# Score maxima from block-diagonal bf16 keys: one 128-row product for two heads, in place of two 64-row products

## The chip, the cores and the metric

The kernel runs on one core of one Trainium2 chip. The metric is the device time of one execution in microseconds. Engines are named as in the profile: PE (TensorE matmul), PEld (TensorE weight load), DVE (VectorE), ACT (ScalarE), POOL (GpSimd), SP (SyncE, which only issues DMAs here).

## The reference

Two layers of cross attention and feed-forward on x of 32 x 128 x 128, with a context of 32 x 77 x 128. Only the first attention is touched by the change: 16 heads of width 64, rotary embedding on queries and keys, a mask of 128 x 77 per batch.

```
Q = (q @ Wq).reshape(b, ql, 16, 64)
K = (k @ Wk).reshape(b, kl, 16, 64)
V = (v @ Wv).reshape(b, kl, 16, 64)
Q, K = (rope(Q), rope(K))
attn = jnp.einsum('bqhd,bkhd->bhqk', Q / scale, K)
attn = jnp.where(mask[:, None, :, :] == 0, -INF, attn)
attn = jax.nn.softmax(attn, axis=-1)
out = jnp.einsum('bhqk,bkhd->bqhd', attn, V).reshape(b, ql, 16 * 64)
return out @ Wo
```

## The kernel before

The program is written out by hand, engine by engine, with semaphores. The first attention takes the 32 batches in 16 pairs. A pair p has two slots, one for each of its batches (j = 0 and j = 1); `pairs_loop` writes out pairs 0 and 1, loops over pairs 2 to 13 (two pairs to a turn of the loop), and writes out pairs 14 and 15. The order of work on each engine is fixed by the text of its `slot`. While pair p is being attended to, the queries, keys and values of pair p + 1 are projected.

Channels lie on partitions: a tile of 128 partitions holds two heads, the even one on partitions 0 to 63 and the odd one on 64 to 127; there are 8 tiles.

Scores are computed twice. First in bf16, `score_maxima(b)`, with queries on the rows, only to find each row's maximum: three PSUM banks first receive the mask through three products with the identity (`am`, line 986, over 308, 462 and 462 columns), then 16 products (line 995) add the scores, one for each head, 64 rows by 128 columns of weights (`qb`) and 77 moving columns (`kb`). Even and odd heads are interleaved so that two 64-row products stand side by side. The bank of four heads gets both parities, so its second half waits for its first (`half_done`). DVE then takes the maxima, bank by bank (`maxima`, line 736: two of 6 heads, one of 4). PE transposes them (`turn_maxima`, line 1007), ACT copies the result (`fold`, line 862), and the fp32 scores (`scores`, lines 1017 and 1021) subtract mask and maximum through a product with `fold`.

The bf16 operands are made by ACT: `cast_queries` (line 850) and `cast_keys` (line 858), from the fp32 `qr` and `kr`. For the keys of pair p + 1, all in the slot j = 1 of pair p: PE projects them in three groups of 3, 3 and 2 tiles (line 970); DVE multiplies and shuffles (lines 679, 681); POOL makes `kr` of the groups 0 and 1 (lines 592, 593), having first made the last group of queries (lines 580, 581), whose PSUM input PE produced at the end of the slot j = 0; DVE makes `kr` of the group 2 (line 724); ACT casts each group as it comes, in order. PE goes through the rest of the slot (`scores`, `turn_out`, `out_projection`, `values`, and `project_values(p + 1, 1)`, lines 949 to 951) and then, before `score_maxima` of the next pair's first batch, executes

```
pe.wait_ge(cast_done, 3 * p + 6)
```

that is, it waits for the third cast of the pair. In the prologue the same wait stands ahead of `score_maxima(0)`. Behind it on PE come `score_maxima`, `project_values`, the transposes of pair p + 2, `turn_out`, `turn_maxima`, and the next slot. Line 845 (ACT) copies projected values out of PSUM, behind the casts in ACT's order.

At the start, POOL sets five small constants (lines 561 to 563) and DVE and ACT wait for the semaphore `setup` to reach 5 before their first work.

Of the kernel before, what the change touches and what calls it, by code (L numbers as in the profile page):

```python
# [11 lines left out]
BF16 = mybir.dt.bfloat16  # L12
# [6 lines left out]
B, S, D, KL = 32, 128, 128, 77  # L19
# [3 lines left out]
TILES = H0 * DK0 // 128  # L23
# [4 lines left out]
CROW = 96  # L28
# [373 lines left out]
def layer0_attention(nc, ctx, t):  # L402

    sb = lambda name, shape, dt: ctx.enter_context(nc.sbuf_tensor("a0_" + name, shape, dt))
# [8 lines left out]
    am = [sb(f"am{i}", [S, 2, FOLD], BF16) for i in range(2)]  # L413
# [12 lines left out]
    kr = [sb(f"kr{i}", [128, TILES, 2, KL], F32) for i in range(2)]  # L426
    qb_all = sb("qb", [128, 2 * TILES * 2 * S], BF16)
    qb = [qb_all[:, 2048 * i:2048 * i + 2048].rearrange("p (t j s) -> p t j s", t=TILES, j=2) for i in range(2)]
    kb = [sb(f"kb{i}", [128, TILES, 2, KL], BF16) for i in range(2)]
    vs = [sb(f"vs{i}", [KL, 2, H0, DK0 + 1], F32) for i in range(2)]  # L430
    fold = sb("fold", [FOLD, S], BF16)
    probs = sb("probs", [KL, H0, S], F32)
# [16 lines left out]
    pa, ps, po = bank[0:2], bank[2:5], bank[5:8]  # L449
# [4 lines left out]
    setup = sem("setup")  # L454
    stats_ready, rstd_ready, xhat_ready = sem("stats_ready"), sem("rstd_ready"), sem("xhat_ready")
    a_full, a_free = [sem(f"a_full{i}") for i in range(2)], [sem(f"a_free{i}") for i in range(2)]
    s_full, s_free = [sem(f"s_full{i}") for i in range(3)], [sem(f"s_free{i}") for i in range(3)]
    values_full, normalised, turned_full, turned_in, out_full, out_added = (
        sem(n) for n in ("values_full", "normalised", "turned_full", "turned_in", "out_full", "out_added"))
    roped, k_roped, cast_done, half_done = sem("roped"), sem("k_roped"), sem("cast_done"), sem("half_done")  # L460
# [11 lines left out]

    SM_BANK = (1, 2, 0)
    SM_COUNT = (lambda b: 2 * b, lambda b: 2 * b, lambda b: 4 * b)
    SM_HEADS = ((0, 2, 4, 6, 8, 10), (1, 3, 5, 7, 9, 11), (12, 14, 13, 15))
    SM_ORDER = ((2, 0), (1, 0), (2, 1), (1, 1), (0, 0), (1, 2), (0, 1), (1, 3), (0, 2), (1, 4), (0, 3), (1, 5),
                (0, 4), (2, 2), (0, 5), (2, 3))

    FOLD_COUNT = lambda b: 4 * b + 1
    ST_BANK = (0, 1, 2, 0)  # L480
# [39 lines left out]
    def a_count(p, task):  # L520

        return 6 * p + task[1] + 1 - task[0]
# [35 lines left out]
    def gpsimd(pool, second):  # L558
        steps = Steps(pool, pool_step)
        for i in range(2):  # L560
            nc.gpsimd.memset(am[i][:, :, KL:CROW], 0.0).then_inc(setup, 1)
            nc.gpsimd.memset(vs[i][:, :, :, DK0:DK0 + 1], 1.0).then_inc(setup, 1)
        nc.gpsimd.memset(t["minus_half"][:], -0.5).then_inc(setup, 1)
        pool.wait_ge(setup, 5)

        def pre(p):
            pool.wait_ge(stats_ready, p + 1)
# [51 lines left out]
    def vector(dve, second):  # L619
# [107 lines left out]
        def maxima(b, P, j):  # L727
            for m in range(3):
                bk = SM_BANK[m]
                dve.wait_ge(s_full[bk], SM_COUNT[m](b) + 1)  # L730
                n, first = len(SM_HEADS[m]), CROW + SM_HEADS[m][0]
                if m < 2:
                    rows = am[P][:, j, first:first + 2 * n - 1:2]
                else:
                    rows = am[P][:, j, first:first + 4].rearrange("p (i e) -> p e i", e=2)
                nc.vector.tensor_reduce(rows, ps[bk][:, 0:n * KL].rearrange("p (h k) -> p h k", k=KL),  # L736
                                        AX, ALU.max).then_inc(s_free[bk], 1)

# [15 lines left out]
            nc.vector.tensor_tensor(x[:, b, :], po[2][:, 0:D], x[:, b, :], ALU.add).then_inc(out_added, 1)  # L754

        dve.wait_ge(x_first_in, 16)
        dve.wait_ge(setup, 5)
        masks(0, 0)
        statistics(0)
        normalised_rows(0)  # L760
# [22 lines left out]
        def slot(b, p, P, j, more):  # L783
# [24 lines left out]
            else:  # L808
# [15 lines left out]
                if more:  # L824
                    maxima(b + 1, 1 - P, 0)
# [9 lines left out]
    def scalar(act, second):  # L835
# [16 lines left out]
        def cast_keys(p, P, k):  # L852
            if k < 2:
                act.wait_ge(k_roped, 2 * p + k + 1)
            else:
                act.wait_ge(a_free[K_TASK[k][0]], a_count(p, K_TASK[k]) + 1)
            lo, hi = K_GROUPS[k]
            nc.scalar.copy(kb[P][:, lo:hi], kr[P][:, lo:hi]).then_inc(cast_done, 1)  # L858

        def fold_in(b):  # L860
            act.wait_ge(s_full[0], FOLD_COUNT(b) + 1)
# [14 lines left out]
        act.dma_start(*x_chunk(0)).then_inc(x_first_in, 16)  # L876
        act.dma_start(t["ident"][:], t["c_id"]).then_inc(t["ids_in"], 16)
        act.dma_start(t["identb"][:], t["c_idb"]).then_inc(t["ids_in"], 16)
        act.wait_ge(setup, 5)
        nc.scalar.activation(t["front"].first_silu[0:S, :], t["minus_half"][:, 0:1], ACT.Exp)  # L880
        act.wait_ge(first_weights_in, 32)
        nc.scalar.copy(wq_hi[:], wq[:]).then_inc(weights_split, 1)
# [54 lines left out]
    def tensor(pe, second):  # L937
# [43 lines left out]

        def score_maxima(b, P, j):
            for m in (2, 0, 1):
                bk, n = SM_BANK[m], len(SM_HEADS[m])
                pe.wait_ge(s_free[bk], SM_COUNT[m](b))
                nc.tensor.matmul(ps[bk][:, 0:n * KL].rearrange("p (h k) -> p h k", k=KL), t["identb"][:],  # L986
                                 am[P][:, j:j + 1, 0:KL].broadcast_to([S, n, KL]), start=True, stop=False,
                                 skip_group_check=True)
            for m, i in SM_ORDER:
                h = SM_HEADS[m][i]  # L990
                e = 64 * (h % 2)
                if (m, i) == (2, 2):

                    pe.wait_ge(half_done, b + 1)
                last = nc.tensor.matmul(ps[SM_BANK[m]][:, i * KL:i * KL + KL], qb[P][e:e + 64, h // 2, j, :],  # L995
                                        kb[P][e:e + 64, h // 2, j, :], start=False, stop=True, skip_group_check=True)
                if (m, i) == (2, 1):
                    last.then_inc(half_done, 1)
                if i == len(SM_HEADS[m]) - 1:
                    last.then_inc(s_full[SM_BANK[m]], 1)  # L1000

        def turn_maxima(b, P, j):

# [132 lines left out]
        out_projection(B - 1)  # L1136

    return dict(sync=sync, gpsimd=gpsimd, vector=vector, scalar=scalar, tensor=tensor)


# [980 lines left out]
```

## Time and profile before

| what | value |
|---|---|
| three runs | 737.15, 739.62, 739.86 us; median 739.62 us |
| span of the profiled execution, first to last instruction | 736.9 us |
| median of the runs less that span | 2.7 us |
| PE busy | 94% of the span |
| DVE, ACT, POOL busy | 76%, 55%, 55% |
| mean granted TensorE clock | 0.993 |

The profiled execution has no time of its own beside its span in what is shown; the 2.7 us by which the runs' median exceeds it is what lies before the first and behind the last instruction, and the spread of the runs. Times below are microseconds from the span's start unless marked ns.

### The profile page before, as it was taken

How to read it: one execution, taken by the hardware profiler on the slowest of the kernel's cores; microseconds unless marked ns; L12 is line 12 of the kernel's file. 1: busy time of each engine (PE TensorE's matmuls, PEld its weight loads, DVE VectorE, ACT ScalarE, POOL GpSimd, SP SyncE). 2: the span in 40 equal slices, each digit the busy share in tenths (PEclk: the TensorE clock that was granted, in tenths of full speed). 3: DMA queues.
4: the chain of work that ended last, by engine and by line, in shares of the span. 5: the costliest groups of instructions: out<-in, count | busy, mean ns of one | idle time of the engine just before them, and what ended most of it. 6: DMA issues, size and time to landing. Idle time of an engine off the chain costs nothing.

```text
span 736.9 us, 24302 instructions
## 1 busy us (share of the span) xinstructions
PE 695.7 (94%) x9267; PEld 574.1 (78%) x9272; DVE 561.1 (76%) x1633; ACT 407.2 (55%) x902; POOL 403.7 (55%) x496
## 2 busy tenths in 40 slices
PE   3789999999999999999999999999999999997785
PEld 3578888888888888888888887788888888875544
DVE  5676786786786786787787675777887888887996
ACT  2344554544544544545544544556666766766896
POOL 3474574484484474475466452546556565633775
PEclk9899999999999999999999999999999999999999
DMA  9400000000000000000000000000000000000011
GB/s 264 115 9 12 9 3 11 10 0 9 9 0 9 9 0 9 9 0 9 9 0 0 1 2 11 10 7 11 7 9 4 9 4 4 5 2 1 22 44 52
DMA packets 23682, 13.04 MB, mean 18 GB/s; under 512 B 6560, under 2 KB 22768, under 8 KB 23632
## 3 DMA queue, kind: packets, MB, share of 16 engines
q1 hardware_dynamic: 22816, 12.00, 6.1%
q8 instruction: 33, 0.54, 0.3%
q10 hardware_dynamic: 816, 0.36, 0.2%
q14 instruction: 17, 0.14, 0.1%
HBM read 10.25 MB, written 2.10 MB: 17 GB/s over the span
## 4 chain that ended last, share of the span: by engine, by line
PE 83%; DVE 9%; issue 3%; ACT 3%; DMA 1%; POOL 0%; ACTq 0%; SPq 0%; DVEq 0%
PE bank L1017 9%; PE bank L1033 9%; PE bank L1053 8%; PE bank L1648 6%; PE bank L949 5%; PE bank L1021 5%; PE bank L970 4%; PE bank L1681 4%; PE bank L951 4%; PE bank L950 4%; PE bank L1044 4%; PE bank L986 2%; PE bank L1666 2%; PE bank L995 2%; DVE f_h_max L1898 2%
## 5 line engine op out<-in xcount | busy, mean ns | idle before, releaser
L580 POOL TENSOR_TENSOR a_turned<-a_turned,a_rope 128x512 f32<-128x512 f32 x63 | 80.7, 1280 | 175.8 <-DVE a_turned L668 175.8
L867 ACT ACTIVATE a_probs<-bank 77x512 f32<-77x512 f32 x128 | 70.8, 590 | 64.9 <-PE bank L1021 64.0
L845 ACT COPY a_vs<-bank 77x512 f32<-77x512 f32 x64 | 37.4, 584 | 101.5 <-PE bank L951 101.5
L665 DVE TENSOR_TENSOR a_straight<-bank,a_rope 128x512 f32<-128x512 f32 x63 | 43.4, 689 | 58.3 <-PE bank L951 54.5
L581 POOL TENSOR_TENSOR a_qr<-a_straight,a_turned 128x512 f32<-128x512 f32 x64 | 82.3, 1286 | 4.9
L1017 PE MATMUL bank<-a_qr,a_kr 64*77 64x128 f32 x1024 | 71.4, 279 | 2.2 <-ACT a_probs L867 0.3
L1017 PEld LDWEIGHTS bank<-a_qr,a_kr 64*77 64x77 f32 x1024 | 56.5, 145 | 16.4 <-ACT a_fold L862 8.6
L1033 PE MATMUL bank<-a_vs,a_probs 77*64 77x65 f32 x2048 | 67.0, 223 | 0.4 <-DVE x_all L754 0.4
L1033 PEld LDWEIGHTS bank<-a_vs,a_probs 77*64 77x64 f32 x2048 | 62.4, 137 | 4.5 <-DVE x_all L754 0.6
L1053 PE MATMUL bank<-a_wo,a_oTn 128*128 128x128 f32 x512 | 64.0, 278 | 0.0
L736 DVE TENSOR_REDUCE a_am<-bank 128x6 bf16<-128x462 f32 (+1 forms) x96 | 50.3, 581 | 14.2 <-PE bank L995 14.2
L1053 PEld LDWEIGHTS bank<-a_wo,a_oTn 128*128 128x128 f32 x512 | 59.9, 192 | 1.0
L850 ACT CAST a_qb<-a_qr 128x512 bf16<-128x512 f32 x64 | 39.4, 618 | 23.5 <-POOL a_qr L581 23.2
L668 DVE STREAM_SHUFFLE a_turned<-bank 128x512 f32<-128x512 f32 x63 | 46.2, 733 | 0.0
L970 PE MATMUL bank<-a_ctxT,a_wk 128*128 128x154 f32 x256 | 45.0, 312 | 0.7 <-ACT a_vs L845 0.7
L1380 DVE TENSOR_REDUCE a_max_m<-bank 128x8 f32<-128x512 f32 x64 | 41.1, 684 | 5.1 <-PE bank L1629 4.6
L1518 ACT ACTIVATE a_qr<-bank 128x512 f32<-128x512 f32 (+1 forms) x96 | 43.8, 538 | 1.0 <-PE bank L1666 1.0
L949 PE MATMUL bank<-a_xT_hi,a_wq_hi 128*128 128x256 f32 x128 | 40.0, 313 | 3.0 <-DVE a_turned L668 1.6
L1021 PE MATMUL bank<-a_fold,a_fold_w 112*77 112x128 bf16 x512 | 41.1, 223 | 0.0
L593 POOL TENSOR_TENSOR a_kr<-a_k_straight,a_k_turned 128x462 f32<-128x462 f32 x32 | 38.5, 1202 | 4.3 <-DVE a_k_turned L688 1.9
L858 ACT CAST a_kb<-a_kr 128x462 bf16<-128x462 f32 (+1 forms) x48 | 24.2, 533 | 27.8 <-POOL a_kr L593 27.7
L873 ACT COPY a_oTn<-bank 128x512 f32<-128x512 f32 x64 | 35.5, 582 | 7.2 <-PE bank L1044 7.2
(277 smaller groups left out, 1890.2 us busy)
## 6 DMA issues: line engine op xcount, KB each, us to landing
out<-x_all SPq DMA_DIRECT2D x16, 128.0 KB, 1.8
x_all<-in_x_dram SPq DMA_DIRECT2D x7, 256.0 KB, 6.5
a_ctx_in<-in_ctx SPq DMA_DIRECT2D x16, 77.0 KB
a_mask_in<-in_mask SPq DMA_DIRECT2D x16, 77.0 KB
a_wv<-in_ctx SPq DMA_DIRECT2D x16, 77.0 KB
a_wq<-in_Wq SPq DMA_DIRECT2D x1, 512.0 KB, 4.9
a_wk<-in_Wk SPq DMA_DIRECT2D x1, 512.0 KB, 6.3
a_wv<-in_Wv SPq DMA_DIRECT2D x1, 512.0 KB, 7.2
```

The source lines that it names most:

```text
L580: steps.link(nc.gpsimd.tensor_tensor(tv, tv, rope[:, 1:2, :].broadcast_to([128, 4, S]), ALU.mult))
L581: nc.gpsimd.tensor_tensor(qr[P][:, 2 * k:2 * k + 2, :, :].rearrange("p t j s -> p (t j) s"), sv, tv, ALU.subtract if made else ALU.add).th ...
L668: nc.vector.stream_shuffle(turned[k % 3][:], pv, mask=[lane ^ 1 for lane in range(32)]).then_inc(a_free[bk], 1)
L736: nc.vector.tensor_reduce(rows, ps[bk][:, 0:n * KL].rearrange("p (h k) -> p h k", k=KL), AX, ALU.max).then_inc(s_free[bk], 1)
L867: nc.scalar.activation(probs[:, 4 * g:4 * g + 4, :], ps[ST_BANK[g]][0:KL, :].rearrange("p (h s) -> p h s", s=S), ACT.Exp).then_inc(s_free[ ...
L949: nc.tensor.matmul(out, lhs_hi, rhs_hi, start=True, stop=False)
L970: last = nc.tensor.matmul(pa[bk][:, 2 * KL * i:2 * KL * i + 2 * KL], wk[:, 128 * (lo + i):128 * (lo + i) + 128], ctxT[:], start=True, stop ...
L1017: nc.tensor.matmul(ps[ST_BANK[g]][0:KL, i * S:(i + 1) * S], kr[P][e:e + 64, h // 2, j, :], qr[P][e:e + 64, h // 2, j, :], start=i == 0, st ...
L1021: last = nc.tensor.matmul(ps[ST_BANK[g]][0:KL, i * S:(i + 1) * S], fold_w[:, h, :], fold[:], start=False, stop=True, skip_group_check=True)
L1033: last = nc.tensor.matmul(po[r][rows, VW * i:VW * (i + 1)], probs[:, PROBS_SLOT[h], rows], vs[P][:, j, h, :], start=True, stop=True)
L1053: last = nc.tensor.matmul(po[2][:, 0:D], oTn[:, i, :], wo[:, i, :], start=i == 0, stop=i == TILES - 1)
L1648: return nc.tensor.matmul(SCORES[g][:, i * S:(i + 1) * S], keys[P][FEATURES[half], j, 128 * tile:128 * tile + 128], q1[P][FEATURES[half], ...
```

## The change

The bf16 keys `kb` become block diagonal: for each tile, a first block of 77 columns holds the even head's keys on partitions 0 to 63 and zero below, and a second block holds zero above and the odd head's keys on partitions 64 to 127. One product of 128 rows by 154 columns then gives both heads' scores. The 16 products of a batch become 8, the banks hold consecutive heads, and the three banks are finished one after the other instead of together. `half_done` is no longer waited for. Each cast of keys becomes two, one for each half of the partitions. POOL sets both `kb` buffers to zero once at the start (128 partitions by 2464 bf16 elements each), ahead of `setup` reaching 7.

```diff
-    kb = [sb(f"kb{i}", [128, TILES, 2, KL], BF16) for i in range(2)]
+    kb = [sb(f"kb{i}", [128, TILES, 2, 2, KL], BF16) for i in range(2)]
...
-    SM_HEADS = ((0, 2, 4, 6, 8, 10), (1, 3, 5, 7, 9, 11), (12, 14, 13, 15))
...
+    SM_TILES = (range(0, 3), range(3, 6), range(6, 8))
...
+            nc.gpsimd.memset(kb[i][:], 0.0).then_inc(setup, 1)
         nc.gpsimd.memset(t["minus_half"][:], -0.5).then_inc(setup, 1)
-        pool.wait_ge(setup, 5)
+        pool.wait_ge(setup, 7)
...
-                n, first = len(SM_HEADS[m]), CROW + SM_HEADS[m][0]
-                if m < 2:
-                    rows = am[P][:, j, first:first + 2 * n - 1:2]
-                else:
-                    rows = am[P][:, j, first:first + 4].rearrange("p (i e) -> p e i", e=2)
+                first, n = CROW + 2 * SM_TILES[m][0], 2 * len(SM_TILES[m])
+                rows = am[P][:, j, first:first + n]
...
-            nc.scalar.copy(kb[P][:, lo:hi], kr[P][:, lo:hi]).then_inc(cast_done, 1)
+            for e in range(2):
+                last = nc.scalar.copy(kb[P][64 * e:64 * e + 64, lo:hi, :, e, :], kr[P][64 * e:64 * e + 64, lo:hi])
+            last.then_inc(cast_done, 1)
...
-            for m, i in SM_ORDER:
-                h = SM_HEADS[m][i]
-                e = 64 * (h % 2)
-                if (m, i) == (2, 2):
-
-                    pe.wait_ge(half_done, b + 1)
-                last = nc.tensor.matmul(ps[SM_BANK[m]][:, i * KL:i * KL + KL], qb[P][e:e + 64, h // 2, j, :],
-                                        kb[P][e:e + 64, h // 2, j, :], start=False, stop=True, skip_group_check=True)
-                if (m, i) == (2, 1):
-                    last.then_inc(half_done, 1)
-                if i == len(SM_HEADS[m]) - 1:
-                    last.then_inc(s_full[SM_BANK[m]], 1)
+            for m in range(3):
+                for i, tile in enumerate(SM_TILES[m]):
+                    last = nc.tensor.matmul(ps[SM_BANK[m]][:, 2 * KL * i:2 * KL * i + 2 * KL], qb[P][:, tile, j, :],
+                                            kb[P][:, tile, j].rearrange("p e k -> p (e k)"), start=False, stop=True,
+                                            skip_group_check=True)
+                last.then_inc(s_full[SM_BANK[m]], 1)
```

## Rows read from the trace of the kernel before

**Rows 1.** The page: busy times, and the chain that ended last by engine.

```profile
PE 695.7 (94%) x9267; PEld 574.1 (78%) x9272; DVE 561.1 (76%) x1633; ACT 407.2 (55%) x902; POOL 403.7 (55%) x496
...
PE 83%; DVE 9%; issue 3%; ACT 3%; DMA 1%; POOL 0%; ACTq 0%; SPq 0%; DVEq 0%
```

**Rows 2.** Chain that ended last, 134 to 145 us: start, us, what.

```profile
141.14 0.48 PE bank L995 x16
```

**Rows 3.** Timeline by form, 138.5 to 144.5 us (start, duration, engine, line).

```profile
137.78 1.18 POOL L593 TENSOR_TENSOR a_kr<-a_k_straight,a_k_turned 128x462 f32<-128x462 f32 x1
...
138.99 0.93 ACT L858 CAST a_kb<-a_kr 128x462 bf16<-128x462 f32 x2 [1.70 <-POOL a_kr L593]
...
140.43 0.24 PEld L986 LDWEIGHTS bank<-a_am,identb 128*128 128x128 bf16 x3 [0.32 <-issue]
140.44 0.70 PE L986 MATMUL bank<-a_am,identb 128*128 128x308 bf16 x3
...
141.07 0.55 PE L995 MATMUL bank<-a_kb,a_qb 64*128 64x77 bf16 x16
...
141.54 0.45 PE L949 MATMUL bank<-a_wv_hi,a_ctxT_hi 128*77 128x512 f32 x1
...
141.62 1.57 DVE L736 TENSOR_REDUCE a_am<-bank 128x6 bf16<-128x462 f32 x3 [0.52 <-PE bank L995]
...
143.52 0.22 PE L1007 MATMUL bank<-identb,a_am 128*112 128x128 bf16 x1
```

**Rows 4.** Timeline, 128.9 to 131.2 us: what starts POOL's run.

```profile
131.01 1.27 POOL L580 TENSOR_TENSOR a_turned<-a_turned,a_rope 128x512 f32<-128x512 f32 x1 [0.75 <-DVE a_turned L668]
```

**Rows 5.** Groups by form, ACT line 858: busy us, mean ns, idle before.

```profile
L858 ACT CAST a_kb<-a_kr 128x462 bf16<-128x462 f32 x32 | 18.5, 577 | 27.7 <-POOL a_kr L593 27.7
...
L858 ACT CAST a_kb<-a_kr 128x308 bf16<-128x308 f32 x16 | 7.1, 443 | 0.1
```

**Rows 6.** Chain, 476 to 480 us: bf16 products of full height, 128 columns.

```profile
478.22 0.56 PE bank L1666 x10
```

**Rows 7.** Timeline, 112.3 to 113.6 us: the pair before.

```profile
111.98 0.93 ACT L858 CAST a_kb<-a_kr 128x462 bf16<-128x462 f32 x2 [1.70 <-POOL a_kr L593]
...
113.37 0.50 PE L986 MATMUL bank<-a_am,identb 128*128 128x308 bf16 x2
```

**Rows 8.** Timeline, 57 to 58.9 us: batch 2, written out.

```profile
57.14 0.93 ACT L858 CAST a_kb<-a_kr 128x462 bf16<-128x462 f32 x2 [1.70 <-POOL a_kr L593]
...
58.57 0.50 PE L986 MATMUL bank<-a_am,identb 128*128 128x308 bf16 x2
```

**Rows 9.** Timeline, 84 to 86.5 us: batch 4.

```profile
84.04 1.12 ACT L858 CAST a_kb<-a_kr 128x462 bf16<-128x462 f32 x2 [1.60 <-POOL a_kr L593]
...
86.31 0.50 PE L986 MATMUL bank<-a_am,identb 128*128 128x308 bf16 x2
```

**Rows 10.** Timeline, 27.5 to 30.2 us: batch 0, the prologue.

```profile
27.87 1.00 ACT L858 CAST a_kb<-a_kr 128x462 bf16<-128x462 f32 x2 [1.20 <-POOL a_kr L593]
...
28.93 0.70 PE L986 MATMUL bank<-a_am,identb 128*128 128x308 bf16 x3 [1.81 <-ACT a_kb L858]
```

**Rows 11.** Groups, POOL, 0 to 2 us: the memsets of the start.

```profile
L562 POOL MEMSET a_vs<- 77x32 f32 x2 | 0.3, 151 | 0.0
L561 POOL MEMSET a_am<- 128x38 bf16 x2 | 0.3, 128 | 0.3 <-POOLq L2110 0.3
L2110 POOL MEMSET const-bfloat16-1.0<- 128x1 bf16 x1 | 0.1, 101 | 0.0
```

**Rows 12.** Timeline, 0 to 62 us: the start on POOL and DVE.

```profile
0.98 0.10 POOL L563 MEMSET minus_half<- 128x4 f32 x1
...
4.61 0.24 DVE L625 TENSOR_SCALAR a_am<-a_mask_in 128x154 bf16<-128x154 int32 x1 [4.61 <-DMA a_mask_in<-in_mask]
...
10.03 0.42 DVE L655 TENSOR_TENSOR a_xT_lo<-bank,a_xT_hi 128x256 fp32r<-128x256 f32 x1
```

**Rows 13.** Line 736: who waited for it (us, times).

```profile
  PE bank L1007: 2.2, 3
```

**Rows 14.** Stretches: busy us by engine, PEclk, DMA.

```profile
30.00:36.60 6.60, 6.17 (x31) 3.92 (x29) 3.07 (x9) 1.55 (x5) 0.07 (x1) 0.50 0.15 41
```

More of the change, by code:

```diff
@@ L474, in layer0_attention @@
     SM_COUNT = (lambda b: 2 * b, lambda b: 2 * b, lambda b: 4 * b)
-    SM_HEADS = ((0, 2, 4, 6, 8, 10), (1, 3, 5, 7, 9, 11), (12, 14, 13, 15))
-    SM_ORDER = ((2, 0), (1, 0), (2, 1), (1, 1), (0, 0), (1, 2), (0, 1), (1, 3), (0, 2), (1, 4), (0, 3), (1, 5),
-                (0, 4), (2, 2), (0, 5), (2, 3))
+    SM_TILES = (range(0, 3), range(3, 6), range(6, 8))
     FOLD_COUNT = lambda b: 4 * b + 1
@@ L756, in vector @@
         dve.wait_ge(x_first_in, 16)
-        dve.wait_ge(setup, 5)
+        dve.wait_ge(setup, 7)
         masks(0, 0)
@@ L878, in scalar @@
         act.dma_start(t["identb"][:], t["c_idb"]).then_inc(t["ids_in"], 16)
-        act.wait_ge(setup, 5)
+        act.wait_ge(setup, 7)
         nc.scalar.activation(t["front"].first_silu[0:S, :], t["minus_half"][:, 0:1], ACT.Exp)
@@ L983, in score_maxima @@
             for m in (2, 0, 1):
-                bk, n = SM_BANK[m], len(SM_HEADS[m])
+                bk, n = SM_BANK[m], 2 * len(SM_TILES[m])
                 pe.wait_ge(s_free[bk], SM_COUNT[m](b))
```

## The prediction, made before the change was run

> **What bounds the kernel now.** I read the page first: PE is busy 94% of the span, and the chain that ended last is 83% PE [rows 1]. Then the chain in order of time through a settled pair: from 60 us to 436 us it is nearly all PE, and the products that the change replaces stand on it in every batch [rows 2]. So in the first attention a nanosecond on PE, or a wait of PE, costs a nanosecond. Next I looked for what PE nearly waits for. The timeline of one pair [rows 3] shows two near misses: the third cast of the keys ends at 138.99 + 0.93 = 139.92 and PE takes up line 986 at 140.44, 0.52 later; the maxima end at 141.62 + 1.57 = 143.19 and PE takes up line 1007 at 143.52, 0.33 later. The reader should see in the first that ACT starts the second cast 0.03 after POOL's row ends (137.78 + 1.18 = 138.96), having idled 1.70 before it: ACT has time, but not at that place.
>
> **PE's own work.** Now, from line 986's first start to the product behind line 995 is 141.54 - 140.44 = 1.10, of which line 995 takes 0.47 and line 986 0.63 [rows 3]. Full-height bf16 products of 128 columns go at 0.56/10 = 0.056 each, 0.44 ns a column [rows 6]. The identity products have 308 + 462 + 462 = 1232 columns, 0.54 at that rate; the 0.09 left is lost where full height gives way to 64 rows. Afterwards nothing changes height: 0.54 + 8 x 154 columns (0.54) = 1.08 against 1.10. With rounding I take -0.03 a batch, x 32 = -1.0. Bounds: 0 to -0.06 a batch (the second if all of the 0.09 and some of the like at the far end comes back on top), so 0 to -2, unless the loss at the change of height stays (a rival below).
>
> The Trainium skill (TensorEngine Tiling (Array Packing), Key Properties) says that a change of tiling mode drains the array; the 0.09 agrees. The same skill speaks against the change (TensorE: Matmul & The Clock Gate, Why this matters for your kernels): products of few rows in separate row groups run concurrently. By concurrency alone the 16 products would be 8 x 77 columns, 0.27, and the new ones 0.54: +0.27 a batch, +8.6 in all. The row gives them 0.47 with losses at the edges, so most of that price is paid already.
>
> **The casts.** Three casts a pair (577, 577, 443 ns, rows 5) become six. Halving the partitions halves no free dimension: each half still streams 462 or 308 elements a partition, so I take the full duration for each. Two casts in a row overlap by 577 + 443 - 930 = 90 ns [rows 3, 5]. Group 0 is doubled in ACT's idle 1.70 and costs nothing. Groups 1 and 2 cannot start before POOL's kr: the last of four casts ends (577 - 90) + (443 - 90) = 0.84 later. I use 0.83. Does the cover of 0.52 hold? PE needs some time from the cast's end to line 986. In the prologue, where it really waited, it was 28.93 - 28.87 = 0.06 [rows 10]. In the loop the wait's threshold, and those of the three waits behind it, are worked out by the sequencer between; the weight load of line 986 shows 0.32 of "issue" ahead of it [rows 3]. I take 0.20, between the two and nearer the second since the loop's code is that of the second row. Stall = 0.83 + 0.20 - cover. The cover is 0.52 in one pair and 113.37 - 112.91 = 0.46 in the next [rows 3, 7], alternating through the loop: 0.51 and 0.57, mean 0.54. Twelve pairs of the loop: +6.5. Bounds with 0.06 and 0.32: 0.40 and 0.66 a pair, 4.8 and 7.9.
>
> Outside the loop: batch 2 has a cover of 58.57 - 58.07 = 0.50 and thresholds that are constants, so 0.83 + 0.06 - 0.50 = +0.4 [rows 8]. Batch 4 has 86.31 - 85.16 = 1.15: nothing [rows 9]; batch 30 looks like it: nothing. Batch 0 waits already: +0.8 less some 0.05 because its third cast now starts behind DVE's kr: +0.75 [rows 10].
>
> Is such a stall won back? Behind the waiting PE stand the maxima, the values, turn_out, the next slot, hence the query projections of the next pair. POOL's run that ends in kr starts from a DVE shuffle of the last query group, after an idle 0.75 [rows 4], and DVE waits there for PE. So the late side hangs on PE as well: all slides together, and the next pair stalls again. Casts that run 0.83 longer push the copy of values (line 845) too, but PE's projection that it waits for ends later than the casts do. Not won back.
>
> **The maxima.** The first bank is full after 3 products of 8 instead of at the end, so DVE starts some 0.25 earlier. Line 1007 waited for DVE 3 times in the whole run, 2.2 in total [rows 13]; elsewhere PE comes 0.33 later anyway [rows 3]. I count one batch: -0.25. Bounds 0 and -0.75.
>
> **The start.** Two memsets of 2464 bf16 a partition go ahead of `setup`. Nearest row: 38 elements of bf16 in 128 ns against 1 element in 101 ns: 0.73 ns an element; the strided f32 one gives (151 - 101)/31 = 1.6 [rows 11]. Hence 1.9 to 4.1 each; the first is the same instruction and type, and I take 2.1. POOL's constants ended at 1.08; now at 5.3. DVE's first work starts at 4.61, released by a DMA [rows 12]: +0.7 late. Does it pass on? At 10.03 DVE subtracts xT_hi as soon as it has it, and PE's first projection waits for that; the path through DVE's first rows, PE's transposes and ACT's three casts ends there with no slack. So +0.7. Bounds: +0.3 and +4.7.
>
> **Sum.** -1.0 + 6.5 + 0.4 + 0.75 - 0.25 + 0.7 = +7.1. On the profiled span, 736.9 + 7.1 = 744.0; the runs' median lies 2.7 above that span, and 739.6 + 7.1 = 746.7, which I predict.
>
> **The rivals.**
> 1. *The casts stay hidden* (not slower). If a cast on 64 partitions costs half, or the six overlap better, the last ends less than 0.26 to 0.32 later (cover less 0.20), and that is the point from which it decides. For it: ACT is 45% idle, and no row shows a cast on 64 partitions at partition 64. Against it: 577 ns for 462 columns and 443 for 308 show that the time goes by columns. Time: -1.0 - 0.25 + 0.7 + 0.2 = about 739.3, no change. Chance 0.12.
> 2. *The array's change of height still costs*, or the concurrency of the old products was worth more than the rows let me see: the 0.09 and its like at the far end stay, +0.12 a batch rather than -0.03, so +4.8 on the forecast: 751.5. Against it: three full-height products follow one another at the column rate. Chance 0.06.
> 3. *The start costs most*: memsets at 1.6 ns an element (+4.0), or the later work meets the clock differently: in 30.0 to 36.6 us the granted clock was at the lower level, 1.2 GHz, 6.6 long, after PE had idled before line 986 [rows 10, 14], and another half of such a stretch would cost 1.7 to 3.3. 749 to 751. Chance 0.09.
> 4. *The maxima were on the path after all*: the 0.25 counts in every batch, 31 x 0.25 = 7.8 back, and the casts' loss is cancelled: 739. Against it: rows 13. Chance 0.04.
>
> The forecast itself, 743.5 to 749, keeps 0.65; 0.04 is for a gain I don't see.
>
> **How the numbers follow.** A measurement of this kernel can tell about 0.5%, 3.7 us, from no change; three runs before spread over 2.7. Slower by more than that is above 743.3: the forecast (0.65 less a little, for its lower edge with a low run), rivals 2 and 3 and nothing else, 0.79. Same: rivals 1 and 4 and that lower edge, 0.17. Faster: 0.04. The range: low bounds of all terms give -2 + 4.8 + 0.4 + 0.75 - 0.75 + 0.3 = +3.5, 743.1, less 1.6 for a low draw of the runs: 741.5. High: 7.9 in the loop, no gain on PE, +1 at the start, +10.0, 749.7; with a part of rival 3, 751.
>
> **What would show it.** Casts of 64 partitions at 577 and 443 ns, six a pair; PE's line 986 with an idle of about 0.5 released by ACT a_kb in 12 pairs of the loop, about 0.4 at batch 2, none at batches 4 and 30; the 8 products 0.067 apart, with 1.07 to 1.08 from line 986 to the next line; the period of a pair up from 27.07 (140.44 - 113.37, rows 3, 7) to about 27.55; DVE's first row near 5.3. It is wrong if the half casts take 300 ns, if PE shows no idle at line 986, or if the sequencer's 0.20 is 0.

## The result and the profile after

| | before | changed |
|---|---|---|
| median of 6 runs each, us | 739.79 (737.15 to 743.01) | 747.77 (747.09 to 749.23) |
| span of the profiled execution, us | 736.9 | 745.3 |
| mean granted TensorE clock | 0.993 | 0.995 |

The ratio is 1.0108, with a 95% interval of 1.0081 to 1.0136: 8.0 us slower. The prediction was 746.7 us, +7.1. Two of its terms were off, in opposite directions, and half cancel. Executions of one kernel also differ in the clock: three of the changed kernel's took 747.1 to 747.3 us at a mean granted clock of 0.995, and two took 749.2 at 0.985.

The page of the changed kernel, against [rows 1]:

```profile
span 745.3 us, 23821 instructions
PE 694.7 (93%) x9016; PEld 579.4 (78%) x9016; DVE 561.2 (75%) x1633; ACT 434.5 (58%) x950; POOL 407.9 (55%) x498
PE 38%; issue 26%; POOL 24%; DVE 9%; ACT 3%; POOLq 1%; ACTq 0%; DVEq 0%
```

PE was 83% of the chain and is 38% of it now, though PE's busy time fell by only 1.0 us. POOL has 24% where it had none: PE now waits, pair after pair, for something that leads back through ACT to POOL. That does not make POOL the engine that bounds the kernel: it is busy 55% as before, and the 26% of "issue" are mostly POOL's own idle time between the pairs (10.89 us from 139.61 in the chain of this pair). ACT's busy time is up by 27.3.

The timeline of the changed kernel over the same place of the same pair as [rows 3] (start, duration, engine, line; in brackets the idle time before and what ended it):

```profile
139.24 1.18 POOL L592 TENSOR_TENSOR a_kr<-a_k_straight,a_k_turned 128x462 f32<-128x462 f32 x1
140.45 2.12 ACT L855 CAST a_kb<-a_kr 64x462 bf16<-64x462 f32 x4 [1.10 <-POOL a_kr L592]
141.66 0.40 PE L949 MATMUL bank<-a_wv_hi,a_ctxT_lo 128*77 128x512 f32 x1
142.59 0.58 ACT L841 COPY a_vs<-bank 77x512 f32<-77x512 f32 x1
142.69 0.25 PEld L984 LDWEIGHTS bank<-a_am,identb 128*128 128x128 bf16 x3 [1.11 <-issue]
142.69 0.70 PE L984 MATMUL bank<-a_am,identb 128*128 128x308 bf16 x3 [0.64 <-ACT a_kb L855]
143.63 1.57 DVE L732 TENSOR_REDUCE a_am<-bank 128x6 bf16<-128x462 f32 x3 [1.08 <-PE bank L989]
143.73 0.44 PE L947 MATMUL bank<-a_wv_hi,a_ctxT_hi 128*77 128x512 f32 x1
```

Line 984 is line 986 of before, 989 is 995, 855 is 858. Three readings. The four casts behind POOL's row take 2.12 where the two took 0.93: 1.19 more. PE starts line 984 at 142.69, 0.12 after the casts end (140.45 + 2.12 = 142.57). And from the start of line 949 to line 984 there is 1.03. Where PE waits for nothing, as in batch 30, written out behind the loop, that is 446.53 - 446.30 = 0.23:

```profile
446.30 0.40 PE L949 MATMUL bank<-a_wv_hi,a_ctxT_lo 128*77 128x512 f32 x1
446.53 0.70 PE L984 MATMUL bank<-a_am,identb 128*128 128x308 bf16 x3
```

So the stall is 1.03 - 0.23 = 0.80 (0.81 as the mean of the loop's twelve pairs), not the 0.64 in the bracket, which counts from a modelled end of line 949. The count of who ended the idle time at line 984 (us and times, of which 14 times are PE's own and 4 the weight loads') and the casts by form (busy, mean ns, idle before), against [rows 5]:

```profile
  ACT a_kb L855: 16.2, 18
```

```profile
L855 ACT CAST a_kb<-a_kr 64x462 bf16<-64x462 f32 x64 | 37.2, 581 | 18.5 <-POOL a_kr L592 18.2
L855 ACT CAST a_kb<-a_kr 64x308 bf16<-64x308 f32 x32 | 14.4, 451 | 0.6
```

The pair's period, from the same line two pairs in a row:

```profile
115.00 0.70 PE L984 MATMUL bank<-a_am,identb 128*128 128x308 bf16 x3 [0.66 <-ACT a_kb L855]
...
170.38 0.70 PE L984 MATMUL bank<-a_am,identb 128*128 128x308 bf16 x3 [0.65 <-ACT a_kb L855]
```

142.69 - 115.00 = 27.69 and 170.38 - 142.69 = 27.69, against 140.44 - 113.37 = 27.07 [rows 3, 7]. Over the loop, from batch 6 to batch 28, the means are 27.70 and 27.05 (before, 27.03 and 27.07 take turns).

### The profile page after: what moved, and what is told of

Read it like the earlier page. It is cut to its first block, busy times and chain, and to the rows that moved or that the text cites. A ratio compares the mean times of both kernels' runs of the same rounds, so it can differ in the third digit from the quotient of the medians.

```text
span 745.3 us, 23821 instructions
## 1 busy us (share of the span) xinstructions
PE 694.7 (93%) x9016; PEld 579.4 (78%) x9016; DVE 561.2 (75%) x1633; ACT 434.5 (58%) x950; POOL 407.9 (55%) x498
## 4 chain that ended last, share of the span: by engine, by line
PE 38%; issue 26%; POOL 24%; DVE 9%; ACT 3%; POOLq 1%; ACTq 0%; DVEq 0%
POOL a_turned L579 9%; POOL a_qr L580 8%; PE bank L1640 5%; PE bank L1673 4%; POOL a_k_turned L591 4%; PE bank L1658 2%; DVE f_h_max L1890 2%; POOL a_kr L592 2%; PE bank L1009 2%; PE bank L1045 1%; PE bank L1614 1%; PE bank L1025 1%; PE bank L1599 1%; PE bank L1704 1%; PE bank L1691 1%
## 5 line engine op out<-in xcount | busy, mean ns | idle before, releaser
L732 DVE TENSOR_REDUCE a_am<-bank 128x6 bf16<-128x462 f32 (+1 forms) x96 | 50.3, 579 | 18.8 <-PE bank L989 17.2
L855 ACT CAST a_kb<-a_kr 64x462 bf16<-64x462 f32 (+1 forms) x96 | 51.6, 538 | 19.1 <-POOL a_kr L592 18.2
L1510 ACT ACTIVATE a_qr<-bank 128x512 f32<-128x512 f32 (+1 forms) x96 | 43.8, 538 | 1.0 <-PE bank L1658 1.0
```

Source lines behind the costliest of these rows:

```text
L855: last = nc.scalar.copy(kb[P][64 * e:64 * e + 64, lo:hi, :, e, :], kr[P][64 * e:64 * e + 64, lo:hi])
L1510: nc.scalar.activation(probs[:, 4 * g:4 * g + n, :], SCORES[g].rearrange("p (t s) -> p t s", s=S), ACT.Exp).then_inc(s_free[g], 1)
```

## The experiments

The theory on trial is the prediction's: PE's new products cost no more than the old ones, and all the loss in the loop is PE waiting at the head of the maxima for a longer chain of casts. The rivals: the new products or the clock cost time, the loss is in the start, or the casts would have been hidden. Chain, stall and period in the table are in us and are means over the loop. The chain is the time from the start of the first cast behind POOL's last kr to the end of the last one. The period is that from line 984 (or its like) to the next pair's, the stall is taken as above.

| | chain of casts behind POOL's kr | stall | period | ratio to before |
|---|---|---|---|---|
| before | 0.93 | 0 | 27.05 | |
| changed | 2.12 | 0.81 | 27.70 | 1.0108 |
| e1, three full casts, new products | 0.94 | 0 | 26.89 | 0.993 |
| e2, old products, full casts twice | 1.76 | 0.47 | 27.54 | 1.0085 |
| e3, old products, casts in halves | 2.09 | 0.80 | 27.86 | 1.0142 |
| e7, changed, halves in another order | 1.87 | 0.58 | 27.47 | 1.0082 |
| e4, changed, DVE casts the odd halves, memsets moved | 0.94 | 0 | 26.89 | 0.9932 |
| e6, as e4, memsets not moved | 0.94 | 0 | 26.89 | 0.9947 |
| e5, changed, memsets moved | 2.11 | 0.83 | 27.71 | 1.0127 |
| e8, changed again | 2.11 | 0.82 | 27.71 | 1.0114 |

In the loop the granted clock is 1.00 in every kernel's profile, so chain, stall and period can be compared directly. The ratios also hold what happens near the start, where PE spends some stretches at 1.2 GHz that differ from kernel to kernel; the texts on e1, e2, e3 and e5 give them.

### e1: the new products with the old casts

Each cast is one instruction again and fills the even block on all partitions; the odd block stays zero. What comes out are maxima of the sum of two heads' scores, so this kernel leaves out the separation of heads; PE's instructions are those of the changed kernel.

```diff
-            for e in range(2):
-                last = nc.scalar.copy(kb[P][64 * e:64 * e + 64, lo:hi, :, e, :], kr[P][64 * e:64 * e + 64, lo:hi])
-            last.then_inc(cast_done, 1)
+            nc.scalar.copy(kb[P][:, lo:hi, :, 0, :], kr[P][:, lo:hi]).then_inc(cast_done, 1)
```

> The changed kernel with one cast of full height per group of keys, into the even block only (the odd heads' block stays zero and the even block's lower half holds the odd head's keys, so the maxima are those of a sum of two heads). The products, the banks and the memsets stay as changed. Theory A (the loss is the chain of casts behind POOL's last kr): in the loop no wait of PE for the keys, period of a pair 27.07 less the gain of the products, which in the changed kernel's rows is 1.11 - 1.03 and 1.11 - 1.07, so about 26.95; with 0.75 of start kept, 0.998 of the kernel before, 738 us. Rival B (the loss lies in the products of full height or in the memsets and the clock after them): the time stays near the changed kernel's, 1.011 of before, 747 to 748 us.

Measured 735.19 us (734.74 to 737.58) against 740.61, ratio 0.993 [0.9903, 0.9957]: faster than the kernel before, and by more than expected. The timeline of e1:

```profile
136.13 1.18 POOL L592 TENSOR_TENSOR a_kr<-a_k_straight,a_k_turned 128x462 f32<-128x462 f32 x1
137.34 0.93 ACT L854 CAST a_kb<-a_kr 128x462 bf16<-128x462 f32 x2 [1.68 <-POOL a_kr L592]
138.78 0.70 PE L982 MATMUL bank<-a_am,identb 128*128 128x308 bf16 x3
```

The casts end at 138.27 and PE comes 0.51 later without a wait, the cover of [rows 3]. The target's stride (blocks of 77 in 154) costs next to nothing: 0.93 here, 0.94 in the mean of the loop, where it was 0.93. The period is 0.17 shorter than before, so the products are a gain of 0.17 a pair, some 2.7 us over 16 pairs.

That is half of the 5.4 us between the medians. The profiled span is 3.6 shorter than before's (733.3 against 736.9), although PE's first projection comes 0.76 later; at batch 1, behind a single round of products, e1 is already 1.59 ahead. What the rows show to differ there is the clock: e1's PE runs at 1.2 GHz from 18.3 to 25.1 and from 28.5 to 31.9, before's from 29.9 to 36.7. The rest of the 5.4 lies in before's other executions: three of the twelve, at a mean granted clock of 0.979, took 743.4 us, and the three at 0.990 or 0.993 took 738.2 to 739.4.

### e2 and e3: the old products with more casts

e2 casts each group twice at full height, the second time into a tile that nothing reads.

```diff
+    kx = [sb(f"kx{i}", [128, TILES, 2, KL], BF16) for i in range(2)]
...
-            nc.scalar.copy(kb[P][:, lo:hi], kr[P][:, lo:hi]).then_inc(cast_done, 1)
+            nc.scalar.copy(kb[P][:, lo:hi], kr[P][:, lo:hi])
+            nc.scalar.copy(kx[P][:, lo:hi], kr[P][:, lo:hi]).then_inc(cast_done, 1)
```

> The kernel before, with each cast of keys followed by a second one of full height from the same source into an unused tile; nothing else changes, output as the reference. Theory A: slower. If a second cast follows the first as closely as group 2 followed group 1 before (0.48 after 577 ns, that is 90 ns of overlap), the third group ends 0.84 later, PE stalls about 0.48 in 12 pairs of the loop, +7, ratio 1.009. If two casts in a row don't overlap, as in the changed kernel, 1.19 later, stall about 0.83, +11 to 12, ratio 1.015 to 1.017. Rival B: no change, since the products are the old ones: within 0.3%.

e3 casts each group in two halves of the partitions, into the old layout.

```diff
-            nc.scalar.copy(kb[P][:, lo:hi], kr[P][:, lo:hi]).then_inc(cast_done, 1)
+            for e in range(2):
+                last = nc.scalar.copy(kb[P][64 * e:64 * e + 64, lo:hi], kr[P][64 * e:64 * e + 64, lo:hi])
+            last.then_inc(cast_done, 1)
```

> The kernel before, with each cast of keys cut into two of 64 partitions each, written without gaps into the old tile; output as the reference. It separates the height of a cast from the strided target: if 64 partitions at a time (or the second at partition 64) is what removes the overlap, casts start 0.58 to 0.60 apart here and in the changed kernel, but 0.48 apart in the run with doubled casts of full height; if it is the strided target, here they start 0.48 apart. Theory A: +11 to 12 us (1.015) in the first case, +7 (1.009) in the second. Rival B: no change.

e2: 747.13 us (745.45 to 749.82), ratio 1.0085 [1.0054, 1.0116]. e3: 751.76 (749.36 to 753.95), 1.0142 [1.0111, 1.0173]. The same number of casts, of the same duration each, and yet 4.6 us apart. The timeline of ACT in e2, and PE's line 988 behind it:

```profile
142.69 0.58 ACT L859 CAST a_kb<-a_kr 128x462 bf16<-128x462 f32 x1 [1.22 <-POOL a_kr L594]
143.17 0.57 ACT L860 CAST a_kx<-a_kr 128x462 bf16<-128x462 f32 x1
143.65 0.45 ACT L859 CAST a_kb<-a_kr 128x308 bf16<-128x308 f32 x1
144.00 0.44 ACT L860 CAST a_kx<-a_kr 128x308 bf16<-128x308 f32 x1
144.35 0.57 ACT L846 COPY a_vs<-bank 77x512 f32<-77x512 f32 x1
...
144.58 0.70 PE L988 MATMUL bank<-a_am,identb 128*128 128x308 bf16 x3 [0.30 <-ACT a_kx L860]
```

And of e3:

```profile
143.15 2.09 ACT L859 CAST a_kb<-a_kr 64x462 bf16<-64x462 f32 x4 [1.11 <-POOL a_kr L593]
...
145.37 0.70 PE L988 MATMUL bank<-a_am,identb 128*128 128x308 bf16 x3 [0.63 <-ACT a_kb L859]
```

In e2 a cast starts 0.48 after the one before, though that lasts 0.58: they overlap by 0.09, and the four end 1.76 after the first starts (1.75 by the rounded rows), 0.83 more than two do. That is the prediction's figure, and in e2 it holds. In e3 the four take 2.09. They start 0.59, 0.60 and 0.46 apart: no overlap at any change from one half of the partitions to the other. e3 has the changed kernel's chain without its products, and its period and ratio are the highest of all.

The two medians also hold something that is not the casts. Both profiled executions have a second stretch at 1.2 GHz, from 43.6 to 50.4 in e2 and from 43.8 to 50.6 in e3, where the kernel before has none. A window of e2:

```profile
43.60:50.40 6.80, 6.80 (x78) 6.00 (x79) 2.89 (x8) 1.55 (x4) 3.26 (x3) 0.50 0.01 2
```

Before's granted clock in it is 1.00. From batch 1 to batch 2 both fall behind before by 3.57 (in e3 0.70 of it is a stall for the casts at batch 2; in e2 PE waits there for DVE instead). From batch 0 to batch 1 both had gained 1.4, with a first stretch of 3.4 in place of 6.8. So of the 9.2 by which e2's span is longer than before's, the stalls of the loop are 5.8. The theory rests on the periods, not on how near the ratios came to what was expected.

The Trainium skill (ScalarE: Activation LUTs, What ACT_TABLE_LOAD costs) gives an activation with immediate scale and bias 186 ns + 0.833 ns an element and says that ones back to back overlap by about 93 ns. e2's rows agree with both (571 and 443 ns by it, 0.09 overlap); the halves of e3 agree with the duration (577 and 449 ns for the first of each group) and not with the overlap, and there the measurement decides.

### e7: one change of half in place of three

The four casts behind POOL's row in the order group 1 lower, group 2 lower, group 2 upper, group 1 upper.

```diff
+        def cast_half(p, P, k, e):
+            lo, hi = K_GROUPS[k]
+            return nc.scalar.copy(kb[P][64 * e:64 * e + 64, lo:hi, :, e, :], kr[P][64 * e:64 * e + 64, lo:hi])
...
-            for e in range(2):
-                last = nc.scalar.copy(kb[P][64 * e:64 * e + 64, lo:hi, :, e, :], kr[P][64 * e:64 * e + 64, lo:hi])
-            last.then_inc(cast_done, 1)
+            if k == 2:
+                return
+            act.wait_ge(k_roped, 2 * p + k + 1)
+            cast_half(p, P, k, 0)
+            if k == 1:
+                act.wait_ge(a_free[K_TASK[2][0]], a_count(p, K_TASK[2]) + 1)
+                cast_half(p, P, 2, 0)
+                cast_half(p, P, 2, 1).then_inc(cast_done, 1)
+            cast_half(p, P, k, 1).then_inc(cast_done, 1)
```

> The changed kernel, with the last four casts of a pair in the order even half of group 1, even half of group 2, odd half of group 2, odd half of group 1. The same six casts on ACT and the same data; only the number of changes from one half of the partitions to the other falls from three to one. Theory A2 (two casts in a row overlap by 90 ns as long as both lie on the same half; a change of half costs the overlap and a little more, which is why my 0.84 became 1.19): starts 0.49, 0.46 and 0.35 apart in place of 0.60, 0.60 and 0.47, last end 1.88 behind POOL's kr in place of 2.15, the stall down by about 0.25 a pair, 3 to 4 us less than the changed kernel: 1.006 to 1.007 of before. Rival A3 (casts of 64 partitions never overlap): starts 0.58 to 0.60 apart, no difference to the changed kernel, 1.011.

745.6 us (743.81 to 746.54), ratio 1.0082 [1.0056, 1.0108]; the changed kernel, run again beside it (e8), 747.62 and 1.0114. The timeline of e7:

```profile
139.63 1.87 ACT L850 CAST a_kb<-a_kr 64x462 bf16<-64x462 f32 x4 [1.10 <-POOL a_kr L592]
...
141.63 0.70 PE L989 MATMUL bank<-a_am,identb 128*128 128x308 bf16 x3 [0.39 <-ACT a_kb L850]
```

The same four instructions in another order take 1.87 in place of 2.12, and starts at 0.49 (no change of half), 0.46 (change, behind a cast of 0.45) and 0.355 (no change) apart. So it is the change of half that loses the overlap. PE's period falls by 0.23 with it (27.70 to 27.47).

The copy of values that ACT does behind the casts, on 77 partitions from partition 0, shows which property counts. In e2 it follows a cast on all 128 partitions and starts 0.09 before that ends (144.35, against 144.00 + 0.44). In the changed kernel it follows a cast on partitions 64 to 127 and starts 0.02 behind its end (142.59 against 142.57). Two instructions of different height overlap where both start at partition 0, so these rows speak for the first partition, not the height.

### e4: the odd halves of the late groups on DVE

```diff
...
-            for e in range(2):
+            for e in range(2) if k == 0 else (0,):
                 last = nc.scalar.copy(kb[P][64 * e:64 * e + 64, lo:hi, :, e, :], kr[P][64 * e:64 * e + 64, lo:hi])
...
+        def cast_odd_keys(p, P):
+            for k in (1, 2):
+                if k == 1:
+                    dve.wait_ge(k_roped, 2 * p + 2)
+                else:
+                    dve.wait_ge(a_free[K_TASK[2][0]], a_count(p, K_TASK[2]) + 1)
+                lo, hi = K_GROUPS[k]
+                nc.vector.tensor_copy(kb[P][64:128, lo:hi, :, 1, :], kr[P][64:128, lo:hi]).then_inc(odd_cast, 1)
...
                     pe.wait_ge(cast_done, 3 * p + 6)
+                    pe.wait_ge(odd_cast, 2 * p + 4)
```

DVE does this behind `residual` in the slot j = 1, and PE waits for `odd_cast` too. The memsets of `kb` were also moved behind POOL's constants, under a semaphore of their own (e5's edit, below).

> The changed kernel, with the odd heads' casts of groups 1 and 2 given to DVE, between its addition of the residual and its normalisation, where it stood idle 0.41 before, and with the two memsets behind a semaphore of their own that DVE and ACT wait for only ahead of the first casts. Output as the reference. Theory A: the third cast ends where it did before the change, no wait of PE in the loop, no delay at the start; only the products' gain is left: 16 x (0.08 + 0.03) = 1.8 us less than before, ratio 0.998 (0.994 to 1.001, the clock's low stretch at the start may be shorter). If DVE's two casts (0.3 to 0.6 each) make the normalisation or the maxima late, the period of a pair is above 27.07. Rival B: near the changed kernel's time, 1.008 to 1.011.

736.09 us (734.76 to 737.55), ratio 0.9932 [0.9909, 0.9956]: this version computes all that the reference asks and beats both kernels. Its timeline:

```profile
138.30 0.94 ACT L869 CAST a_kb<-a_kr 64x462 bf16<-64x462 f32 x2 [1.10 <-POOL a_kr L593]
138.30 0.63 DVE L734 CAST a_kb<-a_kr 64x462 bf16<-64x462 f32 x2
...
139.74 0.70 PE L999 MATMUL bank<-a_am,identb 128*128 128x308 bf16 x3
140.68 1.57 DVE L742 TENSOR_REDUCE a_am<-bank 128x6 bf16<-128x462 f32 x3
```

DVE does its two in 0.63, inside ACT's 0.94; PE comes 0.50 after ACT ends, with no wait. ACT's two half casts without a change of half take 0.94, like the two full ones: the height of 64 costs nothing by itself. The maxima start at 140.68, 0.94 after line 999, as in the changed kernel (143.63 - 142.69), and no queue behind DVE's two casts moved the period: 26.89, e1's. The profiled span is 734.3, 2.6 shorter than before's; as in e1, the larger difference of the medians is in part the clock of before's other executions.

### e5 and e6: the start

e5 is the changed kernel with only the memsets moved.

```diff
         for i in range(2):
             nc.gpsimd.memset(am[i][:, :, :CROW], 0.0).then_inc(setup, 1)
-            nc.gpsimd.memset(kb[i][:], 0.0).then_inc(setup, 1)
         nc.gpsimd.memset(t["minus_half"][:], -0.5).then_inc(setup, 1)
+        for i in range(2):
+            nc.gpsimd.memset(kb[i][:], 0.0).then_inc(zeroed, 1)
...
+        act.wait_ge(zeroed, 2)
```

> The changed kernel, with the two memsets behind a semaphore of their own, which ACT alone waits for, ahead of the first cast. Output as the reference. Theory A with my term for the start: DVE's first row back at 4.6 from 5.37, PE's first projection back at about 10.6 from 11.37, 0.75 us less than the changed kernel, and the loop's period unchanged at 27.68. In time 747.0 against 747.8, which is at the edge of what the rounds tell. A rival: something else holds the start, and PE's first projection stays at 11.4.

749.29 us (746.9 to 749.49), ratio 1.0127 [1.0101, 1.0152]; e8, the changed kernel beside it, 1.0114 [1.0089, 1.0139]. A gain was expected and there is none. DVE's start in e5:

```profile
4.67 0.69 DVE L625 TENSOR_SCALAR a_am<-a_mask_in 128x154 bf16<-128x154 int32 x1 [4.67 <-DMA a_mask_in<-in_mask]
...
10.53 0.42 DVE L655 TENSOR_TENSOR a_xT_lo<-bank,a_xT_hi 128x256 fp32r<-128x256 f32 x1 [0.72 <-ACT a_xT_hi L837]
```

DVE's first row starts at 4.67, near the 4.61 of before, but takes 0.69 beside POOL's memsets where it took 0.24 [rows 12]:

```profile
1.02 4.24 POOL L563 MEMSET a_kb<- 128x2464 bf16 x2
```

The memsets end at 5.26 and the row at 5.36. In e4, which has the same edit, the row starts at 4.59 and ends at 5.35, behind memsets that end at 5.25. In both it ends 0.10 behind them whenever it started, as if it had been held until they were done. So the row that gates PE's first projection moves back only from 10.79 to 10.53 (10.03 before). What this gave went elsewhere. At batch 0 e5 is 1.62 behind the kernel before, the changed kernel 1.87; at batch 1 they are 2.49 and 0.67 behind. A window of e5 between the two (length, busy us of PE, PEld, DVE, ACT, POOL, granted clock, DMA):

```profile
33.50:36.60 3.10, 2.50 (x9) 1.41 (x8) 1.10 (x5) 0.75 (x2) 0.00 (x0) 0.50 0.03 8
```

And of e8:

```profile
33.50:36.60 3.10, 2.46 (x16) 1.39 (x17) 1.34 (x6) 0.98 (x4) 0.00 (x0) 0.88 0.03 8
```

From 33.5 to 36.6 e5's PE runs at 0.50, 1.2 GHz, and does 9 products; e8's does 16 at 0.88. e5's stretches at 1.2 GHz near the start last 6.8 us from 18.8 and 10.2 from 29.0, e8's 3.4 from 30.9. The medians agree with that: five of e5's six executions ran at a mean granted clock of 0.985 to 0.990 and took 749.1 to 749.5 us; the one at 0.995 took 746.9, against 747.3 of e8's at that clock. A gain of 0.3 to 0.4 from the memsets' place is not excluded, but the clock hides it.

e6 is e4 without e5's edit: DVE's odd casts, and the memsets ahead of `setup` as in the change.

> The run with the odd halves of groups 1 and 2 on DVE, but with the memsets ahead of the setup semaphore as in the change. It takes the two edits of that run apart. Theory A: nearly all of the gain is the casts', so 0.994 of the kernel before against 0.993 for both edits; the start 0.75 later, the period 26.88 as there. Rival: the memsets' place was worth more than 0.75 (through the clock's stretch), then 0.998 or above.

735.73 us (733.87 to 737.23), ratio 0.9947 [0.9926, 0.9968], against e4's 0.9932 [0.9909, 0.9956]. The intervals overlap, the period is the same, 26.89, and both have the same stretches at 1.2 GHz (6.8 and 3.4 long): where the memsets stand makes no measurable difference.

### e8: the changed kernel again

> The changed kernel itself, on the same chip as the three above, to compare them with it directly: 1.011 of the kernel before, 1.008 to 1.014.

747.62 us (747.3 to 749.31), ratio 1.0114 [1.0089, 1.0139], span 745.5: the result repeats.

## Why the prediction was right, and where its terms were off

The offsets of the changed kernel's profile against before's, at the first product of the maxima of each batch named:

| where | offset, us | what came on top |
|---|---|---|
| PE's first projection | +0.76 | the start |
| batch 0 | +1.87 | casts, +1.11 |
| batch 1 | +0.67 | clock, and one round of products, -1.20 |
| batch 2 | +1.13 | PE waits for DVE's residual, +0.70; maxima and products, -0.25 |
| batch 4 | +1.00 | casts, +0.69; a like wait of before's is gone, -0.68; products, -0.14 |
| batch 6 | +1.63 | casts less products |
| batch 28 | +8.73 | 11 pairs of the loop, +7.10 |
| end of the span | +8.4 | no stall from batch 30 on |

**The mechanism** was right in every run: the loop's loss is stall less products. Where PE waits in the loop it starts 0.13 behind the last cast; in the kernel before it comes 0.49 behind it in the mean, 0.46 and 0.52 by turns, which is the cover. These and the chain give each kernel's stall: 2.12 + 0.13 - (0.93 + 0.49) = 0.83 for a measured 0.81, and in the same way 0.80 for e3's 0.80, 0.58 for e7's 0.58 and 0.47 for e2's 0.47. Stall less 0.17 (where the products are new) gives each period within 0.02: 27.05 + 0.81 - 0.17 = 27.69, 27.05 + 0.58 - 0.17 = 27.46, 27.05 - 0.17 = 26.88. That such a stall isn't won back later is shown too: e3's period is up by 0.81, its whole stall.

**The number** was luck in part. The loop's stall and the products both came out beyond the bounds that were set for them, in opposite directions, and the clock gave back 1.2 that no term had foreseen. With the casts as they came, and the products and the clock as forecast, the sum would have been 3.9 higher, 11.0, and the time 750.6, near the upper end of the range.

**The casts: term mis-sized.** "I use 0.83" was measured at 1.19. Each half takes the full duration, as predicted (581 and 451 ns), but the 0.09 of overlap, read from two full-height casts in a row, is lost where the half of the partitions changes. The sequencer's 0.20 was 0.13. The cover was the 0.49 that the sum goes by (the "0.51 and 0.57, mean 0.54" behind it are the stalls that covers of 0.52 and 0.46 give, not covers). In place of 0.54 a pair it is 0.81, and 12 x 0.81 = 9.7 in place of 6.5, outside the bounds of 4.8 to 7.9: they asked how long PE takes to follow, and never doubted the overlap. Batch 0 cost 1.11 for 0.75, by the same 0.36.

**PE's own products: term mis-sized the other way.** -0.03 a batch was about -0.08, outside the lower bound too. The timeline of PE in the changed kernel, the slot j = 0 of the same pair:

```profile
151.91 0.70 PE L984 MATMUL bank<-a_am,identb 128*128 128x308 bf16 x3
152.98 1.99 PE L1045 MATMUL bank<-a_wo,a_oTn 128*128 128x128 f32 x16
154.81 0.22 PE L999 MATMUL bank<-identb,a_am 128*112 128x128 bf16 x1
```

From line 984 to what follows is 1.07 here and 1.04 above (143.73 - 142.69), where I had 1.08 for both; before it was 1.10 or 1.11 in both slots. And line 1045, out_projection, takes 1.83 to the next line where it took 1.89: the change of height cost something behind the old products too, beyond them. The "like at the far end" that I put into a bound was real: 0.04 + 0.07 + 0.06 = 0.17 a pair, e1's period. -2.7 in place of -1.0. The Trainium skill (TensorEngine Tiling (Array Packing), Key Properties) says that a change of tiling mode drains the array; the rows agree, on both sides of the products.

The sum with measured terms: 0.7 up to batch 1 (start 0.8, casts 1.1, clock -1.2), 0.45 at batch 2 (0.70 - 0.25), casts 0.7 less 0.7 at batch 4, 9.7 in the loop, and -2.5 for the products behind batch 2 make 8.35 against the span's 8.4. Against my 7.1 that is +3.2 and +0.4 from the casts of the loop and of batch 0, +0.3 from those of batches 2 and 4, about -1.5 from the products and -1.2 from the clock.

**Batches 2 and 4: exchanged.** I gave batch 2 the price 0.4 and batch 4 nothing, because its cover was 1.15 [rows 9]. It came the other way: no stall for the casts at batch 2, and 0.69 at batch 4. PE's timeline before, at batch 4:

```profile
82.86 1.62 PE L1033 MATMUL bank<-a_vs,a_probs 77*64 77x65 f32 x48
84.93 0.69 PE L1033 MATMUL bank<-a_vs,a_probs 77*64 77x65 f32 x16 [0.45 <-DVE x_all L754]
85.55 0.45 PE L949 MATMUL bank<-a_wv_hi,a_ctxT_hi 128*77 128x512 f32 x1
```

And in the changed kernel, at batches 2 and 4:

```profile
56.23 1.62 PE L1025 MATMUL bank<-a_vs,a_probs 77*64 77x65 f32 x48
58.33 0.69 PE L1025 MATMUL bank<-a_vs,a_probs 77*64 77x65 f32 x16 [0.47 <-DVE x_all L750]
58.95 0.46 PE L947 MATMUL bank<-a_wv_hi,a_ctxT_hi 128*77 128x512 f32 x1
59.71 0.50 PE L984 MATMUL bank<-a_am,identb 128*128 128x308 bf16 x2
...
83.84 2.09 PE L1025 MATMUL bank<-a_vs,a_probs 77*64 77x65 f32 x64
85.86 0.46 PE L947 MATMUL bank<-a_wv_hi,a_ctxT_hi 128*77 128x512 f32 x1
86.39 0.40 PE L949 MATMUL bank<-a_wv_hi,a_ctxT_lo 128*77 128x512 f32 x1
87.31 0.70 PE L984 MATMUL bank<-a_am,identb 128*128 128x308 bf16 x3 [0.52 <-ACT a_kb L855]
```

PE waits for DVE's residual in the middle of the values. Here too the bracket counts from a modelled end, and the starts give the whole wait. The 64 products take 85.86 - 83.84 = 2.02 where nothing holds them, 85.55 - 82.86 = 2.69 before and 58.95 - 56.23 = 2.72 at batch 2: waits of 0.67 and 0.70. So of before's cover of 1.15 at batch 4, 0.67 was time in which PE itself had waited upstream, and without it 0.48 is left, the cover of the loop. The same wait makes before's pair from batch 2 to batch 4 longer than the usual 27.05: 86.31 - 58.57 = 27.74. In the changed kernel PE waits so at batch 2, where it hides the casts (line 984 follows with no idle), and not at batch 4, where the casts show: 87.31 - 86.39 - 0.23 = 0.69. It isn't simply that the wait moved: in e1, e2, e4, e6 and e7 PE waits for the residual at both batches, in e3 at batch 4 only, with a stall for the casts at batch 2. Why DVE comes late at the one place and not at the other was not tried. Batch 30 had no stall, as predicted, but narrowly: line 984 starts 0.13 behind the casts' end.

**The start** was predicted at +0.7 and came at +0.76, by the steps given:

```profile
0.86 2.15 POOL L561 MEMSET a_kb<- 128x2464 bf16 x1
5.37 0.24 DVE L624 TENSOR_SCALAR a_am<-a_mask_in 128x154 bf16<-128x154 int32 x1 [5.37 <-POOL minus_half L562]
```

2.15 for the 2.1 taken, and DVE's first row at 5.37 for 5.3. What I had not counted is what the clock does with it. Against [rows 14], the changed kernel's window:

```profile
30.00:36.60 6.60, 5.15 (x29) 3.33 (x31) 2.91 (x10) 2.34 (x7) 0.72 (x1) 0.74 0.18 48
```

0.74 in place of 0.50: before, PE ran at 1.2 GHz for 6.8 us from 29.9, now for 3.4 from 30.7, and with it 1.20 of the 1.87 came back by batch 1. That it is the clock rests on the window and the offsets; the stretch was not varied by itself. Nor does the later start alone shorten it: in e1 and e6 PE's first projection comes at the same 11.37, and they run at 1.2 GHz for 6.8 and for 3.4 us.

**The maxima** were predicted at -0.25 for one batch, and the rows show the term. Before, and in the changed kernel, the one long wait of PE for them, behind batch 1:

```profile
43.81 0.23 PE L1007 MATMUL bank<-identb,a_am 128*112 128x128 bf16 x1 [1.73 <-DVE a_am L736]
```

```profile
44.23 0.23 PE L999 MATMUL bank<-identb,a_am 128*112 128x128 bf16 x1 [1.42 <-DVE a_am L732]
```

The wait is 0.31 shorter (1.73 in e2 and e3 too, 1.42 in all kernels with the new products), and from batch 1's line 984 to this row it is 2.66 in place of 2.91.

**The rivals.** That the casts stay hidden (1) is refuted by the idle at line 984 here and in e2 and e3. That the change of height stays (2) is refuted by e1: the new products are a gain of 0.17 a pair. The start (3) cost what was forecast, and the clock behind it gave back 1.2 where the rival had it cost 1.7 to 3.3. The maxima on the path (4) would have given 0.25 a batch; e1's period has no room for it beyond the products' 0.17 a pair.

## What to carry to other kernels

Splitting an instruction by partitions, where it stands between the last producer and the engine that bounds the kernel, costs its full duration again, and an overlap read from two like instructions in a row must not be carried over to two that start at different partitions. Before a piece of work is priced against a cover, look upstream on the same engine: a cover that holds another wait (the 0.67 at batch 4) goes when that wait does not come. Compare periods of the settled loop before totals: here stretches at 1.2 GHz near the start moved the totals by 1 to 3 us, as much as the effects under study. The products themselves gained 0.17 a pair, 2.7 us or 0.4%, and the loss in the loop came from who prepares their operands: half of the late casts on an engine that was free at that moment (e4, e6) turned 1.1% slower into 0.7% or 0.5% faster than before by the medians (0.3% by the profiled spans), with a period 0.17 below before's.

## What was not expected of the hardware

- ACT's casts overlap by 0.09 us with the one before when both start at the same partition, and not at all when the half changes: starts 0.60 against 0.49 apart for 462 elements, 0.46 against 0.355 for 308. Height did not matter: a copy on 77 partitions overlapped by 0.09 with a cast on 128 ahead of it (e2), and not with one on partitions 64 to 127 (changed kernel).
- DVE's copy of the mask, 128 x 154 from int32 to bf16, took 0.24 us alone and 0.69 (e5) and 0.76 (e4) beside POOL's memsets of 128 x 2464 bf16, and ended 0.10 behind them both times. A memset itself took 2.15.
- The stretches at 1.2 GHz near the start differ between kernels whose first projections lie less than 0.8 us apart: 6.8 us in the kernel before, 3.4 in the changed kernel and e8, 6.8 and 3.4 in e1, e4 and e6, 6.8 and 10.2 in e5. What decides it was not tried.
